# A decoder block on one core: cross attention's transposes split into row halves, and its slots put in another order

## What is computed

```python
q = _split_heads(query @ Wq.T + bq)
k = _split_heads(key @ Wk.T + bk)
v = _split_heads(value @ Wv.T + bv)
scores = jnp.einsum('bhqd,bhkd->bhqk', q, k) * scale
scores = jnp.where(mask == 0, NEG_INF, scores)
probs = jax.nn.softmax(scores, axis=-1)
out = jnp.einsum('bhqk,bhkd->bhqd', probs, v)
out = out.transpose(0, 2, 1, 3).reshape(query.shape[0], -1, D_MODEL)
return out @ Wo.T + bo
```

## Time and profile before

| | |
|---|---|
| median of 3 runs | 427.1 us (426.8 to 427.51) |
| the profiled execution's own time | 428.63 us |
| its span, first to last instruction | 426.9 us |
| PE busy | 402.9 us, 94% |
| DVE busy | 252.5 us, 59% |
| ACT busy | 192.5 us, 45% |
| mean granted TensorE clock | 0.992 |
| first score of slot 0 to first score of slot 31 | 160.76 to 314.96 us |

### The profile page before, as it was taken

How to read it: one execution, slowest core, us unless ns; L and a number is a source line. 1 busy time by engine, 2 the same in 40 slices (tenths; PEclk the granted TensorE clock), 3 DMA queues, 4 the chain that set the end, 5 groups by cost and what they waited for, 6 DMA issues and landing times.

```text
span 426.9 us, 12682 instructions
## 1 busy us (share of the span) xinstructions
PE 402.9 (94%) x4986; PEld 284.7 (67%) x4987; DVE 252.5 (59%) x729; ACT 192.5 (45%) x575; POOL 51.2 (12%) x79
## 2 busy tenths in 40 slices
PE   8989999999999788999999999999899999999992
PEld 7857878878787565666666666666565475566661
DVE  1357775856667555666668676768673642244443
ACT  1054462443616526677667656667683101111220
POOL 4010001101011001000001010100100054222333
PEclk9999999999999999999999999999999999999998
DMA  7998100000000013050404040920000013121210
GB/s 250 381 390 239 33 3 3 2 5 2 4 3 2 4 38 134 16 185 3 185 2 185 9 178 2 374 110 2 0 4 2 2 61 100 62 62 58 71 44 25
DMA packets 15255, 34.48 MB, mean 81 GB/s; under 512 B 2381, under 2 KB 9150, under 8 KB 13920
## 3 DMA queue, kind: packets, MB, share of 16 engines
q1 hardware_dynamic: 13952, 30.72, 20.5%
q0 software_dynamic: 1104, 2.76, 1.8%
q10 hardware_dynamic: 144, 0.23, 0.2%
HBM read 27.27 MB, written 6.70 MB: 80 GB/s over the span
## 4 chain that ended last, share of the span: by engine, by line
PE 47%; issue 38%; DVE 9%; ACT 4%; POOL 2%; POOLq 0%; DVEq 0%; ACTq 0%
PE banks L444 9%; PE banks L830 5%; PE banks L923 4%; PE banks L899 4%; PE banks L905 4%; PE banks L466 4%; PE banks L521 3%; PE banks L486 3%; ACT p L984 3%; PE banks L842 3%; PE banks L508 3%; DVE p L1155 2%; DVE pT L1164 1%; DVE nm L1147 1%; POOL xb L377 1%
## 5 line engine op out<-in xcount | busy, mean ns | idle before, releaser
L1285 DVE CUSTOM_DVE_ANT_0 p<-banks,mask 112x375 f32<-112x375 f32 x128 | 62.6, 542 | 28.2 <-PE banks L633 28.1
L1038 ACT ACTIVATE p<-p,nm 112x375 f32<-112x375 f32 x128 | 73.8, 603 | 5.3 <-DVE nm L1285 5.2
L1045 ACT ACTIVATE pT<-banks 128x336 f32<-128x336 f32 x96 | 42.3, 442 | 42.2 <-PE banks L653 41.9
L653 PEld LDWEIGHTS banks<-ident,p 112*128 112x128 f32 (+1 forms) x384 | 38.4, 140 | 28.9 <-issue 22.0
L984 ACT ACTIVATE p<-banks,nm 128x112 f32<-128x112 f32 x128 | 43.2, 363 | 31.5 <-DVE nm L1147 31.5
L653 PE MATMUL banks<-ident,p 112*128 112x112 f32 (+1 forms) x384 | 53.2, 266 | 1.9 <-DVE nm L1285 1.5
L444 PE MATMUL banks<-x2T,arena 128*128 128x224 f32 x256 | 52.5, 361 | 0.0
L444 PEld LDWEIGHTS banks<-x2T,arena 128*128 128x128 f32 x256 | 48.9, 194 | 1.8 <-ACT arena L974 0.2
L359 POOL TENSOR_TENSOR rstd<-veps,minus_half 128x1 f32<-128x1 f32 x14 | 7.7, 551 | 286.1 <-DVE veps L1179 286.1
L1140 DVE TENSOR_SCALAR arena<-banks 128x448 f32<-128x448 f32 x32 | 19.8, 620 | 28.9 <-PE banks L444 28.9
L466 PE MATMUL banks<-arena,x2T 128*32 128x256 f32 (+1 forms) x512 | 29.9, 381 | 1.7 <-issue 1.4
(11 more groups left out here) (144 smaller groups left out, 566.8 us busy)
## 6 DMA issues: line engine op xcount, KB each, us to landing
arena<-in_ug SPq DMA_DIRECT2D x8, 1024.0 KB, 5.7
arena<-in_dn SPq DMA_DIRECT2D x8, 512.0 KB, 6.7
mid<-in_ctxT SPq DMA_DIRECT2D x8, 375.0 KB, 3.3
slots_s<-blank SPq DMA_DIRECT2D x14, 128.5 KB
arena<-in_wqk SPq DMA_DIRECT2D x7, 256.0 KB, 6.1
slots_x<-blank SPq DMA_DIRECT2D x14, 128.0 KB
p<-slots_s SPq DMA_DIRECT2D x9, 128.5 KB, 2.0
kT<-slots_x SPq DMA_DIRECT2D x9, 128.0 KB, 2.1
```

Source lines behind the costliest of these rows:

```text
L653: mm = pe.transpose(PE_T2[r][0:k1 - k0, t * S:(t + 1) * S], p2_rows[:, i % RING, k0:k1], ident[0:S, 0:S])
L1038: act.activation(p2[i % RING], p2[i % RING], ACT.Exp, bias=nm2[:, i % H:i % H + 1], scale=-1.0).then_inc(exp2, 1)
L1045: act.activation(pT2[:, i % RING], PE_T2[r][:, 0:KT * S].rearrange("p (k n) -> p k n", k=KT), ACT.Copy).then_inc(pt2_act, 1)
L1285: v.tensor_tensor_reduce(p2[i % RING], PE_S2[r][0:S, 0:S2], bias[:], 1.0, 3e38, ALU.add, ALU.min, accum_out=nm2[:, i % H:i % H + 1]).then_ ...
```

## The change

- `turn2_(n, p)` now turns a pair of heads (p = 0: heads 0 and 1; p = 1: heads 2 and 3). Each transpose of 112 rows is cut into one of rows 0 to 63 and one of rows 64 to 111 (`HALVES`), which write to two different banks: 24 transposes a slot take the place of 12.
- TensorE's slot n is now: `score2(n)`, the three fillers, `value2(n-2)`, pair 1 of slot n-1, pair 0 of slot n. Pair 0 is so turned in its own slot.
- ScalarE copies both halves of pair 0 and the 64-row half of pair 1, VectorE the 48-row half of pair 1; the last two copies are what `score2` of the next slot waits for.
- Masks and exponentials go in the order of heads 2, 0, 1, 3 (`MASK_ORDER`), so that the filler at place 1 waits for the slot's first mask and not its third.
- `project_q(b // 2 + 1)` for b = 2 and 4 moves from (g, place) = (1, 2) to (2, 0), and `turn_o` of those batches to (2, 2). ScalarE's extra work stands behind its second exponential, `evac_k` now in the slots of g = 0 and 1.
- After slot 31 `out2`, the last pairs and the shared expert's first products stand in another order.

```diff
-        PE_T2 = (bank[4], bank[7], PE_S2[0], PE_S2[1])
+        PE_T2 = ((bank[4], bank[7]), (PE_S2[0], PE_S2[1]))
+        HALVES = ((0, 64), (64, S))
+        MASK_ORDER = (2, 0, 1, 3)
...
-            def turn2_(n, r):
-                pe.wait_ge(exp2, n * STRIPS + r + 1)
-                if n == 0 and r == 0:
+            def turn2_(n, p):
+
+                pe.wait_ge(exp2, n * STRIPS + 3 + p)
+                if n == 0 and p == 0:
                     pe.wait_ge(ot1[0], B)
                     pe.wait_ge(ot1[1], B)
-                elif n == 0 and r == 1:
                     pe.wait_ge(y1, NT)
-                elif r == 0:
-                    pe.wait_ge(pt2_act, n * 3 - 2)
-                elif r == 1:
-                    pe.wait_ge(pt2_act, n * 3 - 1)
+                elif p == 0:
+                    pe.wait_ge(pt2_act, 3 * n - 1)
                 elif n + 1 < SLOTS:
-                    pe.wait_ge(max2, (n + 1) * STRIPS + r - 1)
-                i = n * STRIPS + r
-                for t in range(KT):
-                    k0, k1 = KEYS[t][0], min(KEYS[t][0] + 128, SP)
-                    mm = pe.transpose(PE_T2[r][0:k1 - k0, t * S:(t + 1) * S], p2_rows[:, i % RING, k0:k1], ident[0:S, 0:S])
+                    pe.wait_ge(max2, (n + 1) * STRIPS + 3)
+                for j in range(2):
+                    i = n * STRIPS + 2 * p + j
+                    for t in range(KT):
+                        k0, k1 = KEYS[t][0], min(KEYS[t][0] + 128, SP)
+                        for half, (q0, q1) in enumerate(HALVES):
+                            at = (j * KT + t) * (q1 - q0)
+                            mm = pe.transpose(PE_T2[p][half][0:k1 - k0, at:at + q1 - q0],
+                                              p2_rows[q0:q1, i % RING, k0:k1], ident[q0:q1, q0:q1])
                 mm.then_inc(turn2, 1)
...
-                    pe.wait_ge(max2, n * STRIPS + 3)
+                    pe.wait_ge(max2, n * STRIPS + 1)
...
-                if (g, place) == (1, 2) and b in (2, 4):
+                if (g, place) == (2, 0) and b in (2, 4):
                     pe.wait_ge(k_sb, (b + 2) * KC)
                     project_q(b // 2 + 1)
-                if (g, place) == (2, 0) and b >= 1:
+                if (g, place) == (2, 2 if b in (2, 4) else 0) and b >= 1:
...
             for n in range(SLOTS):
                 score2(n)
-                if n >= 1:
-                    turn2_(n - 1, 0)
-                    turn2_(n - 1, 1)
-                between(n, 0)
-                if n >= 1:
-                    turn2_(n - 1, 2)
-                    turn2_(n - 1, 3)
-                between(n, 1)
-                between(n, 2)
+                for place in range(3):
+                    between(n, place)
+                if n == SLOTS - 1:
+                    out2(NT - 2)
                 if n >= 2:
                     value2(n - 2)
-            out2(NT - 2)
-            turn2_(SLOTS - 1, 0)
-            turn2_(SLOTS - 1, 1)
+                if n >= 1:
+                    turn2_(n - 1, 1)
+                turn2_(n, 0)
             value2(SLOTS - 2)
-            turn2_(SLOTS - 1, 2)
-            turn2_(SLOTS - 1, 3)
...
             shared(0, 0, range(0, 1))
+            turn2_(SLOTS - 1, 1)
+            shared(0, 0, range(1, 2))
             value2(SLOTS - 1)
-            shared(0, 0, range(1, 2))
             turn_x2(NT - 2, bank[1])
+            shared(0, 1, range(0, 1))
             pe.wait_ge(y2, NT - 1)
             turn_o(B - 1)
-            shared(0, 1, range(0, 1))
+            shared(0, 1, range(1, 2))
             turn_on(B - 1)
-            shared(0, 1, range(1, 2))
             logits_first()
...
-                act.wait_ge(turn2, i + 1)
+            def evac_pt(n, p, half):
+
+                act.wait_ge(turn2, 2 * n + p + 1)
                 if n >= 2:
                     act.wait_ge(pv2, n - 1)
-                act.activation(pT2[:, i % RING], PE_T2[r][:, 0:KT * S].rearrange("p (k n) -> p k n", k=KT),
+                i, (q0, q1) = (n * STRIPS + 2 * p) % RING, HALVES[half]
+                act.activation(pT2[:, i:i + 2, :, q0:q1],
+                               PE_T2[p][half][:, 0:2 * KT * (q1 - q0)].rearrange("p (r t n) -> p r t n", r=2, t=KT),
                                ACT.Copy).then_inc(pt2_act, 1)
-
-            def before_exps(n):
-
-                b, g = n // GROUPS, n % GROUPS
...
+                if (g, place) in ((0, 0), (1, 0)) and 1 <= b < B - 1:
+                    evac_k(g, b + 1)
...
             for n in range(SLOTS):
-                before_exps(n)
                 if n >= 1:
-                    evac_pt(n - 1, 0)
+                    evac_pt(n - 1, 0, 0)
+                    evac_pt(n - 1, 0, 1)
+                between(n, -1)
+                exps2(n, 2)
                 exps2(n, 0)
+                between(n, 0)
+                exps2(n, 1)
                 if n >= 1:
-                    evac_pt(n - 1, 1)
-                exps2(n, 1)
-                between(n, 0)
-                if n >= 1:
-                    evac_pt(n - 1, 2)
-                exps2(n, 2)
+                    evac_pt(n - 1, 1, 0)
                 between(n, 1)
                 exps2(n, 3)
-            evac_pt(SLOTS - 1, 0)
-            evac_pt(SLOTS - 1, 1)
-            evac_pt(SLOTS - 1, 2)
+                between(n, 2)
+            evac_pt(SLOTS - 1, 0, 0)
+            evac_pt(SLOTS - 1, 0, 1)
+            evac_pt(SLOTS - 1, 1, 0)
...
             for n in range(SLOTS):
                 between(n, 0)
+                mask_and_max(n, 2)
                 mask_and_max(n, 0)
+                between(n, 1)
                 mask_and_max(n, 1)
-                between(n, 1)
-                mask_and_max(n, 2)
                 between(n, 2)
                 mask_and_max(n, 3)
+                between(n, 3)
                 if n >= 1:
                     evac_pt2(n - 1)
-                between(n, 3)
                 between(n, 4)
             ln2_add(NT - 2)
             ln2_a(NT - 2)
```

More of the change, by code:

```diff
@@ L1036, in exps2 @@
                 i = n * STRIPS + r
-                act.wait_ge(max2, i + 1)
+                act.wait_ge(max2, n * STRIPS + MASK_ORDER.index(r) + 1)
                 act.activation(p2[i % RING], p2[i % RING], ACT.Exp, bias=nm2[:, i % H:i % H + 1], scale=-1.0).then_inc(exp2, 1)
-            def evac_pt(n, r):
-                i = n * STRIPS + r
-                act.wait_ge(turn2, i + 1)
+            def evac_pt(n, p, half):
+                act.wait_ge(turn2, 2 * n + p + 1)
                 if n >= 2:
                     act.wait_ge(pv2, n - 1)
-                act.activation(pT2[:, i % RING], PE_T2[r][:, 0:KT * S].rearrange("p (k n) -> p k n", k=KT),
+                i, (q0, q1) = (n * STRIPS + 2 * p) % RING, HALVES[half]
+                act.activation(pT2[:, i:i + 2, :, q0:q1],
+                               PE_T2[p][half][:, 0:2 * KT * (q1 - q0)].rearrange("p (r t n) -> p r t n", r=2, t=KT),
                                ACT.Copy).then_inc(pt2_act, 1)
-            def before_exps(n):
-                b, g = n // GROUPS, n % GROUPS
[L1051 to L1054, removed]
             def between(n, place):
@@ L1060, in between @@
                     evac_x1(2)
-                if (g, place) == (1, 0) and b == 0:
+                if (g, place) == (1, -1) and b == 0:
                     evac_x1(3)
-                if (g, place) == (1, 0) and 1 <= b < B - 1:
-                    evac_k(1, b + 1)
-                if (g, place) == (3, 0) and b == 0:
+                if (g, place) == (1, 2) and b == 0:
+                    evac_x1(4)
+                if (g, place) == (2, 2) and b == 0:
+                    evac_x1(5)
+                if (g, place) == (3, -1) and b == 0:
                     evac_x1(6)
+                if (g, place) in ((0, 0), (1, 0)) and 1 <= b < B - 1:
+                    evac_k(g, b + 1)
                 if (g, place) == (3, 0) and b >= 1:
@@ L1282, in mask_and_max @@
                 if i >= RING:
-                    v.wait_ge(turn2, i - RING + 1)
+                    v.wait_ge(turn2, 2 * (n - 2) + r // 2 + 1)
                 v.sem_inc(pause, 1)
@@ L1288, in evac_pt2 @@
             def evac_pt2(n):
-                i = n * STRIPS + STRIPS - 1
-                v.wait_ge(turn2, i + 1)
+                v.wait_ge(turn2, 2 * n + 2)
                 if n >= 2:
                     v.wait_ge(pv2, n - 1)
-                v.tensor_copy(pT2[:, i % RING], PE_T2[STRIPS - 1][:, 0:KT * S].rearrange("p (k n) -> p k n", k=KT)).then_inc(pt2_dve, 1)
+                i, (q0, q1) = (n * STRIPS + 2) % RING, HALVES[1]
+                v.tensor_copy(pT2[:, i:i + 2, :, q0:q1],
+                              PE_T2[1][1][:, 0:2 * KT * (q1 - q0)].rearrange("p (r t n) -> p r t n", r=2, t=KT)).then_inc(pt2_dve, 1)
             def evac_ot(b):
@@ L1341, in between @@
                     ln2_b(b - 3)
-                if (g, place) == (1, 4) and b in (2, 4):
+                if (g, place) == (2, 2) and b in (0, 2, 4):
```

(2 more changed lines are left out.)

## The result

The changed kernel takes 441.1 us (median of 4 runs, 436.9 to 442.1), the kernel before 427.0 beside it: a ratio of 1.031, with a 95% interval from 1.024 to 1.038. It is slower, as forecast, and 5.6 us slower than the 435.5 that I gave; that is inside the range and outside the forecast's own 432 to 439.

The account below looks back on a forecast made before the run. TensorE's own order was taken to set the cross-attention slots; slot differences by batch and the tail summed to +8.4 us on the median of 427.1, giving 435.5 us, with a range from 431 to 442.

Parts of the forecast that it names:

- The halves side by side: TensorE's half transposes: both row halves stream at once, so a pair takes 0.06 us against 0.095 for a full transpose.
- The rival of serial halves: Half transposes on TensorE do not run side by side: 441 us at 0.095 a pair, 445 at 0.12; chance 0.14.
- My own account: The main forecast for the whole kernel, 435.5 us with its own range from 432 to 439; chance 0.72.
- The scores' wait for pair 1's copies: End of each slot: the next `score2` waits for ScalarE's copy, 1.2 us from pair 1's start to the scores.
- `out2` behind `evac_on`: Slots of g = 3, batches 2 to 6: `out2` waits for `evac_on` behind the second exponential; 6.3 us for 5.33.
- the sign: What would show the forecast right: `out2` idle ahead of it for about 1.4 us in slots of g = 3.
- The layer norm ahead of g = 1: Slots of g = 1 from batch 3 on: layer norm delays the first mask to 2.1 us; 5.4 for 4.95.
- the chain with `evac_k` in it: Masks and exponentials up to pair 0, with `evac_k` ahead of the third exponential: 4.45 us, deciding slots of g = 1.
- The new order of masks costs nothing either: VectorE's masks: three are done at S + 2.7, ahead of pair 1 in all but batch 7's last two slot kinds.
- F: Time of a slot's fillers on TensorE; a slot was put at 3.0 + F us unless the exponentials' chain decides.
- S: A slot's first score product, the moment from which the forecast counts times in a slot.
- the slots of g = 2 with `project_q`: Batches 2 and 4: `turn_o` waits for the copy of `project_q`, which ends at 3.9 us; slot 6.65 us.

Follow-up runs that it names:

- the two profiles with repeats: Normalised-row transposes repeated in batch 0's second slot: on the changed kernel, 441.0 us; on it plus early values, early `evac_on` and later `evac_k`, 424.75 us.
- the three moves: Changed kernel with values right behind the scores, `evac_on` ahead of the first exponential, `evac_k` behind the third: 424.6 us, 0.994 of the kernel before.

## Why the forecast came out as it did

- **The halves side by side: right.** A pair takes (0.94 - 0.22) / 23 of the steps twice, 0.063; I took 0.06. The rival of serial halves gave 441 to 445, and the time came out at 441.1. By the time alone one would have taken that rival for the cause. The timeline excludes it, since serial streams at 0.095 a pair would put 12 pairs at 1.2 or more.
- **The range held partly by luck.** My own account ended at 439; the top of the range, 442, was there for serial streams, which did not come. What filled the place up to 441.1 are in the main the two terms below that I did not have.
- **The scores' wait for pair 1's copies: right.** 1.18 for 1.2; 0.24 of it is idle time, in some 20 slots (5.0 / 0.24). Slots with g = 0 take 5.05 for 5.15.
- **`out2` behind `evac_on`: right for the slot's length, not for the idle time.** 6.09 for 6.3: `out2` starts 3.13 after the scores (239.05 to 242.18), for 3.35. But it stands idle for 0.25 and not for the 1.4 that I had named as the sign; another 0.52 has moved ahead of `project_v`, to the mask wait below. So `evac_on` alone is worth 0.51 a slot, by the run that moved it. In the last slot `out2` starts 3.35 after the scores (324.61 to 327.96), just as worked out.
- **The layer norm ahead of g = 1: right,** 5.36 for 5.4 (though 5.71 in batch 4), and the chain with `evac_k` in it, 4.36 for 4.45.
- **"The new order of masks costs nothing either": wrong.** I had asked only whether three masks are done ahead of pair 1. The first mask, for which TensorE stands at place 1, I had left out of F, though I had found just such a wait in the g = 2 slots of before. `project_v` cannot start before S + 1.8, and without a first set of transposes ahead of it, `turn_o` or `turn_on` is over before that. This put g = 2 at 4.73 for 4.3, g = 3 of batch 1 at 4.72 for 4.25 and g = 0 of batch 7 at 4.72 for 4.0. Over batches 1 and 7 and three slots with g = 2 it makes about 2.7 us, and with the last slot of batch 0 (4.71 for 4.1, with 0.48 of it ahead of `project_v`) 3.3. The run with the values first shows the cause: the wait goes, and these slots with it.
- **Nothing in the forecast priced the clock.** Two falls of the clock, at 170 and at 327 us, cost about 1.5 us (7.77 for the 6.24 without one) and 1.3 (four products of `out2` 2.04 for 1.13, and the values behind them 1.20 for 0.79).
- Slots that I put too high give some 2.0 back, and the early start 0.5. 8.4 + 3.3 + 2.8 - 2.5 is 12.0, which is what the profiled executions differ by. The 2.0 is what the other terms leave over; most of it is in the slots of g = 2 with `project_q` (6.46 for 6.65) and in those of g = 3 (6.09 for 6.3) and g = 0 (5.05 for 5.15).

The execution with the highest mean clock, 0.993, took 436.9 us, 1.4 above the forecast; those at 0.986 and 0.978 took 440.6 and 441.6 to 442.1.

## What to carry to other kernels

Work that is moved away from behind a wait uncovers that wait: after each removed piece, ask for every semaphore wait left in the stretch what stood ahead of it and now does not. Here 0.25 a slot was gained by a faster transpose and up to 0.8 lost to waits that the transposes in their old places had hidden; moving the values into the gap, and ScalarE's two copies out of two chains, turned 3.1% slower into 0.6% faster. And a time that agrees with a rival's number is no evidence for the rival until its own mark in the trace has been looked for.

## What the runs showed of the hardware that was not expected

The granted clock fell to 0.50, which is 1.2 GHz, in the midst of cross attention, where in its profile the kernel before stayed at 1.00. It did so behind stretches in which TensorE had done little: in the changed kernel 2.82 of 4.30 us ahead of the first fall, and a wait of 2.11 us ahead of the second (the view names a mask for it, but `out2` waits for `evac_on`, the second line):

```profile
327.96 2.04 PE L693 MATMUL banks<-wx,x1T 128*128 128x256 f32 x4 [2.11 <-DVE nm L1281]
327.48 0.34 ACT L1004 ACTIVATE x1T<-banks 128x224 f32<-128x224 f32 x1
329.93 1.20 PE L674 MATMUL banks<-pT,v 128*32 128x112 f32 x24
...
332.29 0.79 PE L674 MATMUL banks<-pT,v 128*32 128x112 f32 x24 [0.28 <-ACT pT L1044]
```

Both kernels have one more fall ahead of cross attention, from 147 to 151 us in the kernel before and from 146 to 150 in the changed one, each behind a wait of 3.03 us.

The Trainium skill says in "TensorE: Matmul & The Clock Gate", Part 1, that half rate is the default and that TensorE's activity lifts it. The runs agree so far as each of these falls came behind a stretch with long waits, and as the clock stayed up at 170 us in the two profiles with repeats. But waits alone do not decide: in the run with the copies of keys moved the same second slot is busy for 2.80 of 4.28 us and the clock stays at 1.00 in the slot behind it; and slot 29 of the three moves is busy for 3.18 of 4.95 us in one profile and 3.19 of 4.95 with the repeats, and only behind the second does the clock fall. What the runs leave open is why a fall then shows up elsewhere, and which execution has how many: the same three moves ran with mean clocks between 0.986 and 0.995, and took 422.5 to 426.4 us.

Half transposes had a price between full products: with sets of them on both sides, `project_k` took 1.46 for 1.28, so that 12 half transposes were no gain over 6 full ones there.
